# A graph layer on one core: edge groups on TensorE in pairs, with one code and one branch per pair

## The chip, the core and the metric

The kernel runs on one core of a Trainium2 chip. The metric is the device time of one execution in microseconds. Times inside the profile are counted from the start of the span. TensorE's granted clock is given as a share of full speed.

## What is computed

One layer of a graph network on x (625 nodes, 256 channels) with 20000 edges sorted by their target node dst. Cut to what matters:

```python
xn = _layernorm(x)
sums   = segment_sum(xn[src], dst, 625)
counts = segment_sum(ones, dst, 625)
aggr   = sums / maximum(counts, 1)
x = x + (aggr @ W_l.T + xn @ W_r.T + b_r) + linear_attention(xn)
x = x + mixture_of_experts(_layernorm(x))
```

The attention has 8 heads of 32 channels (norms of q and k, second-order terms, projection). The last part is a hidden layer of 1024 with gelu, a softmax over 8 experts and the best expert's matrix for each node, times its probability. Everything is computed in one launch.

## The kernel before

All work is written by hand in five programs, one per engine, that meet in semaphores. The nodes stand in T = 5 tiles of 125. The part of interest is the edge stage. It builds a 625 x 625 matrix of edge counts in PSUM, which is later multiplied with xn @ W_l.T. The 20000 edges are 160 chunks of 125 edges, in NG = 32 groups of GC = 5 chunks. For each chunk, two tiles with one row per edge are made: one marks the edge's target node (VectorE, L644, 628 columns), one is a step at its source node (ScalarE for three chunks of five, L480; VectorE for the other two, L647). TensorE multiplies them: for one tile of target nodes, five chunks, each as a product of 501 columns (L928) and one of 126 columns (L930), adding up in PSUM banks 0 to 6. Since the edges are sorted, most groups have targets in one tile of 125 nodes only. Four of the 32 have a second tile (L938, L940).

**The code.** Which tile a group has is known only at run time. GpSimd makes a code for each group (L432 to L449): first tile + 8 x last tile if that is another + 128 if there are more than two. `group(g)` (L919) loads the code of its group into a register with `value_load` (L921), waits until the fills are there (`oh_ready` from VectorE, `steps_ready` from ScalarE), issues the ten products at addresses taken from the register, and then branches: `If(code > 7)` around the second tile, inside it `If(code > 127)` around a loop over the tiles between. A closing product of two columns (L952) adds 1 to `oh_free`.

**The buffers.** `oh` holds OHB = 7 groups. `fill(g)` on ScalarE (L484) and on VectorE (L639) writes buffer g % 7 and first waits for `oh_free` of at least g - 6:

```python
            def fill(g):
                if g >= OHB:
                    act.wait_ge(oh_free, g - OHB + 1)
                step_rows(g, 0, act_steps(g)).then_inc(steps_ready, 1)
```

**The jobs.** Between the groups TensorE does 14 small jobs for the attention in PSUM bank 7. In this order: the sums M over k (L962, 20 products of 129 columns), five times four transposes of q and k (T, L969), four products U (L986), four products N for the norms (L991). Before job n (from the first T on) it waits for `b7_free`, the reading of the job before. M and U are read by VectorE (L704, L714), T and N by ScalarE (L524 and L532). The order on TensorE is: groups 0 to 2, M, groups 3 and 4, T, groups 5 and 6, T, and so on, two groups behind each job (`groups_to`, L955), then group 31. On ScalarE and VectorE the order of fills is set by `groups_past(job)`: behind the reading of job n come the fills of groups 7 + 2n and 8 + 2n. The engine that does not read a job fills without waiting for it. Behind the last group seven products (L996) end the sums in each bank and release everything that follows (`A_done`): the copies out of PSUM (L539, L723), the attention scores (L1017) and the rest.

## Time and profile before

| | |
|---|---|
| median of 3 runs | 276.13 us (275.94 to 276.99) |
| the profiled execution | 274.62 us |
| its span | 272.9 us |
| TensorE products busy | 238.6 us, 87% of the span |
| VectorE busy | 146.2 us, 54% |
| ScalarE busy | 144.0 us, 53% |
| TensorE's granted clock over the span | 0.998 |
| group 0's first product | 31.94 us |
| closing products of the edge stage (L996) | 106.50 us |

The profiled execution is a single one with the profiler on; its time is its own and lies 1.5 us under the median. PE is TensorE's products, PEld its weight loads, DVE VectorE, ACT ScalarE, POOL GpSimd. A busy time of products contains their pipelined ends, so consecutive rows overlap; the distance between two starts is what one product costs. Register operations, branches, waits and the loading of registers have no rows of their own: they show only as the time in which the array has nothing.

### The profile page before, as it was taken

The numbers are of one execution on the slowest core, as the hardware profiler recorded it, in microseconds if no ns is written. First come the engines' busy times: TensorE is split into PE (matmuls) and PEld (weight loads), VectorE is DVE, ScalarE is ACT, GpSimd is POOL, SyncE is SP. The second block draws the span as 40 slices with busy tenths as digits, with TensorE's granted clock in tenths as the row PEclk, the third lists the DMA queues.
The fourth block names the chain that finished last, engine by engine and source line by source line (L and its number), as shares of the span: only waits on it lengthen the run. The fifth ranks groups of instructions, "written<-read, shape, count | busy, mean of one in ns | idle before, by whom it ended". The sixth has DMA issues, their size and how long they took to land.

```text
span 272.9 us, 4760 instructions
## 1 busy us (share of the span) xinstructions
PE 238.6 (87%) x1447; PEld 146.5 (54%) x1448; DVE 146.2 (54%) x418; ACT 144.0 (53%) x213; POOL 29.1 (11%) x57
## 2 busy tenths in 40 slices
PE   7599799879898998788889997699789999999990
PEld 3248465545454544322227885354445558888880
DVE  2897989996999922973014446900460123322221
ACT  2699656899998952788884011432304332333100
POOL 7018000000000003300000000000053000000331
PEclk9999999999999999999999999999999999999999
DMA  4750000000000000059940000020012300000011
GB/s 127 262 199 2 0 4 2 2 6 2 2 2 2 2 2 2 2 213 424 420 179 2 1 0 0 0 113 40 0 38 65 95 0 4 0 1 2 21 37 40
DMA packets 6032, 15.83 MB, mean 58 GB/s; under 512 B 2725, under 2 KB 3784, under 8 KB 4724
## 3 DMA queue, kind: packets, MB, share of 16 engines
q1 hardware_dynamic: 4576, 13.43, 13.2%
q0 software_dynamic: 1280, 1.31, 1.8%
q10 hardware_dynamic: 144, 0.66, 0.6%
q8 instruction: 22, 0.36, 0.6%
q14 instruction: 10, 0.07, 0.1%
HBM read 14.08 MB, written 1.30 MB: 56 GB/s over the span
## 4 chain that ended last, share of the span: by engine, by line
PE 65%; DVE 17%; ACT 11%; issue 3%; DMA 2%; POOL 0%; DVEq 0%; ACTq 0%
PE ps L1193 15%; PE ps L1128 10%; DVE mem L644 9%; PE ps L887 6%; PE ps L1017 6%; ACT qk_sb L548 6%; PE ps L928 5%; PE ps L1089 4%; DVE mem L647 4%; ACT mem L480 3%; PE ps L1176 3%; DMA edges_sb<-in_edges 2%; PE ps L1080 2%; PE ps L1082 2%; PE ps L1099 2%
## 5 line engine op out<-in xcount | busy, mean ns | idle before, releaser
L480 ACT ACTIVATE mem<-ids_m,half_src 125x628 bf16<-125x628 f16 x96 | 69.9, 808 | 4.4 <-DVE half_src L618 3.6
L928 PE MATMUL ps<-mem 125*128 125x501 bf16 x160 | 47.3, 375 | 11.1 <-issue 6.1
L644 DVE TENSOR_SCALAR mem<-node_ids,dst_f 125x628 bf16<-125x628 f16 x160 | 52.5, 382 | 0.0
L1193 PE MATMUL ps<-mem 128*125 x192 | 41.6, 379 | 0.0
L1193 PEld LDWEIGHTS ps<-mem 128*125 128x125 f32 x192 | 35.9, 188 | 5.4
L930 PE MATMUL ps<-mem 125*128 125x126 bf16 x160 | 35.0, 219 | 0.0
L548 ACT ACTIVATE qk_sb<-ps,sc_col 125x626 f32<-125x626 f32 (+1 forms) x40 | 29.1, 778 | 6.3 <-PE ps L1017 6.3
L928 PEld LDWEIGHTS ps<-mem 125*128 x160 | 15.6, 98 | 29.9 <-issue 17.6
L1128 PE MATMUL ps<-xnT,w_sb 128*128 128x512 f32 (+1 forms) x104 | 28.8, 435 | 1.9 <-ACT mem L579 1.9
L647 DVE TENSOR_SCALAR mem<-ids_m,src_f 125x628 bf16<-125x628 f16 x64 | 24.5, 383 | 0.0
L1128 PEld LDWEIGHTS ps<-xnT,w_sb 128*128 128x128 f32 x104 | 15.9, 191 | 14.7 <-issue 12.6
L582 ACT ACTIVATE mem<-ps,b_sb 128x625 f32<-128x625 f32 x14 | 11.0, 783 | 19.9 <-PE ps L1128 19.6
L1017 PE MATMUL ps<-mem 32*125 32x313 f32 (+1 forms) x160 | 16.1, 472 | 5.1 <-ACT qk_sb L548 5.1
L599 ACT COPY mem<-mem 128x1000 f32 x8 | 8.2, 1031 | 19.8 <-PE ps L1193 19.8
L930 PEld LDWEIGHTS ps<-mem 125*128 x160 | 15.5, 97 | 2.7 <-issue 0.6
L858 DVE SCALAR_TENSOR_TENSOR row<-vz,row x12 | 5.8, 485 | 20.0 <-issue 20.0
L463 POOL DMA_INDIRECT rows_sorted<-row,pos x5 | 6.2, 1235 | 89.9 <-issue 89.9
L1037 PE MATMUL ps<-qk_sb,vz 125*32 125x313 f32 (+1 forms) x160 | 14.7, 439 | 0.9 <-ACT qk_sb L548 0.9
L843 DVE COPY mem<-mem 128x500 f32 (+2 forms) x12 | 4.1, 393 | 20.3 <-ACT mem L582 20.0
L1017 PEld LDWEIGHTS ps<-mem 32*125 32x125 f32 x160 | 6.2, 180 | 16.3 <-ACT qk_sb L548 14.4
L887 PE MATMUL ps<-wqkv_sb,xnT 128*125 128x512 f32 (+1 forms) x40 | 14.1, 490 | 0.0
L744 DVE SCALAR_TENSOR_TENSOR yT_sb<-ps,vs,mem 128x313 f32<-128x313 f32 (+1 forms) x4 | 2.2, 544 | 20.1 <-PE ps L1037 20.1
(200 smaller groups left out, 283.6 us busy)
## 6 DMA issues: line engine op xcount, KB each, us to landing
mem<-in_wd SPq DMA_DIRECT2D x8, 1024.0 KB, 13.1
w_sb<-in_w SPq DMA_DIRECT2D x1, 1024.0 KB, 8.6
vz<-in_bd SPq DMA_DIRECT2D x1, 1000.0 KB
wqkv_sb<-in_w_qkv SPq DMA_DIRECT2D x1, 768.0 KB, 4.2
x_all<-in_x ACTq DMA_DIRECT2D x1, 640.0 KB, 4.8
row<-rows_sorted SPq DMA_DIRECT2D x1, 579.7 KB
wlr_sb<-in_w_lr SPq DMA_DIRECT2D x1, 512.0 KB, 6.0
bqk_all<-in_b_qk SPq DMA_DIRECT2D x1, 256.0 KB, 5.2
```

What stands on the lines that cost most here:

```text
L480: ins = nc.scalar.activation(oh[:, g % OHB, 0, j, :], ids_m1[:, :], ACT.Sign, bias=half_src[:, g * GC + j:g * GC + j + 1])
L548: nc.scalar.activation(gsq[:, u % NGB, :, 0:w], ps[0:TP, b:b + 2, 0:w], ACT.Square, bias=sc2_col[0:TP, :]).then_inc(g_ready, 1)
L582: ins = nc.scalar.activation(hT[:, k, :], psf[:, at:at + N], ACT.Gelu, bias=b1_sb[:, k:k + 1])
L644: ins = nc.vector.tensor_scalar(oh[:, g % OHB, 1, j, :], node_ids[:, :], dst_f[:, col:col + 1], None, ALU.is_equal)
L647: ins = nc.vector.tensor_scalar(oh[:, g % OHB, 0, j, :], ids_m1[:, :], src_f[:, col:col + 1], 2.0, ALU.is_ge, ALU.mult)
L887: ins = mm(ps[0:TP, QKV_BANKS[n % 4], lo:hi], xnT[:, c, TP * t:TP * (t + 1)], w[:, c, :], start=(c == 0), stop=(c == KC - 1))
L928: mm(psf[:, bass.ds(first * BANK, TW + 1)], node_of, oh[:, buf, 0, j, 0:TW + 1], start=False, stop=False, skip_group_check=True)
L930: mm(psf[:, bass.ds(first * P + 5 * BANK, AW)], node_of, oh[:, buf, 0, j, TW:N + 1], start=False, stop=False, skip_group_check=True)
L1017: ins = mm(ps[0:TP, 2 * ((2 * u2 + h // 2) % SLOTS) + h % 2, 0:hi - lo], kT[rows, hg, TP * m:TP * (m + 1)], qT[rows, hg, lo:hi], start=Tru ...
L1037: ins = mm(ps[D * h:D * (h + 1), 6 + k % 2, 0:hi - lo], v[:, m, P * hg + D * h:P * hg + D * (h + 1)], gsq[:, (2 * u2 + pr) % NGB, i, 0:hi ...
L1128: ins = mm(psf[:, at + lo:at + hi], w1_sb[:, c, P * k:P * (k + 1)], x2nT[:, c, lo:hi], start=(c == 0), stop=(c == KC - 1))
L1193: ins = mm(ps[0:TP, 4 + n % EB, 0:C], hT_step[:, n % EB, k, :], wd_sb[:, bass.ds(e, 1), k, :], start=(k == 0), stop=(k == KH - 1))
```

## The change

Groups are taken two at a time. GpSimd packs two codes into one number (code of the even group + 256 x code of the odd one), 16 numbers instead of 32, with two more operations. On TensorE `pair(p)` takes the place of `group(g)`: one `value_load`, the ten products of each of the two groups, then one branch that is taken around the extra tiles of both groups unless a bit of 0xF8F8 is set. Inside, `other_tiles` looks at each half by itself. One closing product per pair adds 2 to `oh_free`. FIRST goes from 3 to 4, so two pairs stand ahead of M, one pair behind M and one behind each other job, and no single group is left at the end. The fills' order moves by one group: 8 + 2n and 9 + 2n behind job n (AHEAD = OHB + 1). The waits for `oh_free` keep their values.

The diff:

```diff
--- before.py
+++ after.py
@@ -26,6 +26,7 @@
     NCH = edges.shape[2]
     GC = 5
     NG = NCH // GC
+    NP = NG // 2
     OHB = 7
     OHW = TP * (T - 1) + P
     H = temp.shape[1]
@@ -106,7 +107,8 @@
         two_code = sb("two_code", [1, NG])
         more_code = sb("more_code", [1, NG])
         ones_col = sb("ones_col", [TP, 1], BF16)
-        flags = sb("flags", [1, NG], I32)
+        pair_hi = sb("pair_hi", [1, NP])
+        flags = sb("flags", [1, NP], I32)
         more = sb("more", [1, T, NG], I32)
         at_sb = sb("at_sb", [P, T * N])
         QB = P + 1
@@ -320,17 +322,20 @@
 
 
         QKV_BANKS = (7, 4, 5, 6)
+        PAIR = 256
         JOB_M = 0
         JOB_QKT = JOB_M + 1
         JOB_U = JOB_QKT + T
         JOB_N = JOB_U + 4
         JOBS = JOB_N + 4
-        FIRST = 3
+        FIRST = 4
+        assert NG == 2 * NP and NG == FIRST + 2 * JOBS
+        AHEAD = OHB + 1
         halves = [(hg, hf) for hg in range(2) for hf in range(2)]
 
 
         def groups_past(job):
-            return [g for g in (OHB + 2 * job, OHB + 2 * job + 1) if g < NG]
+            return [g for g in (AHEAD + 2 * job, AHEAD + 2 * job + 1) if g < NG]
 
         def x_bank(j):
             return ps[:, 4 + j, :]
@@ -445,7 +450,10 @@
             step(nc.gpsimd.tensor_scalar(between[:, :, :], between[:, :, :], 0.0, None, ALU.is_gt))
             step(nc.gpsimd.tensor_scalar(tile_of[:, :, :], tile_of[:, :, :], 0.0, None, ALU.is_gt))
             step(nc.gpsimd.tensor_tensor(tile_of[:, :, :], tile_of[:, :, :], between[:, :, :], ALU.mult))
-            nc.gpsimd.tensor_copy(flags[:, :], two_code[:, :])
+            by_pair = two_code[:, :].rearrange("o (p w) -> o p w", w=2)
+            step(nc.gpsimd.tensor_scalar(pair_hi[:, :], by_pair[:, :, 1], float(PAIR), None, ALU.mult))
+            step(nc.gpsimd.tensor_tensor(pair_hi[:, :], pair_hi[:, :], by_pair[:, :, 0], ALU.add))
+            nc.gpsimd.tensor_copy(flags[:, :], pair_hi[:, :])
             nc.gpsimd.tensor_copy(more[:, :, :], tile_of[:, :, :]).then_inc(flags_ready, 1)
 
             pool.wait_ge(A_done, 1)
@@ -516,7 +524,8 @@
                     act.wait_ge(sums_ready, 1)
                     nc.scalar.activation(nrm[:, :, 0, :], nrm[:, :, 0, :], ACT.Sqrt, scale=SC2)
                     nc.scalar.activation(nrm[:, :, 1, :], nrm[:, :, 1, :], ACT.Sqrt).then_inc(std_ready, 1)
-            fill(T + 1)
+            for g in range(T + 1, AHEAD):
+                fill(g)
 
             fill_past(JOB_M)
             for j in range(T):
@@ -695,7 +704,7 @@
                 scale = nrm[:, t].rearrange("p w (b h) -> p (w b) h", h=HG)[:, :, :, None]
                 nc.vector.tensor_tensor(q4, q4, scale.broadcast_to([TP, 4, HG, D]), ALU.mult
                                         ).then_inc(qk_scaled, 1)
-            for g in range(3, OHB):
+            for g in range(3, AHEAD):
                 fill(g)
 
             dve.wait_ge(b7_full, JOB_M + 1)
@@ -916,45 +925,40 @@
                 zeroed(b)
             pe.wait_ge(flags_ready, 1)
 
-            def group(g):
+            def products(g, tile):
                 buf = g % OHB
-                code = pe.value_load(flags[0:1, g:g + 1], min_val=0, max_val=2048)
-                first = nc.s_assert_within(code & 7, min_val=0, max_val=T - 1,
-                                           skip_runtime_bounds_check_because="each group has edges, each of a tile")
-                pe.wait_ge(oh_ready, g + 1)
-                pe.wait_ge(steps_ready, g + 1)
                 for j in range(GC):
-                    node_of = oh[:, buf, 1, j, bass.ds(first * TP, P)]
-                    mm(psf[:, bass.ds(first * BANK, TW + 1)], node_of, oh[:, buf, 0, j, 0:TW + 1],
+                    node_of = oh[:, buf, 1, j, bass.ds(tile * TP, P)]
+                    mm(psf[:, bass.ds(tile * BANK, TW + 1)], node_of, oh[:, buf, 0, j, 0:TW + 1],
                        start=False, stop=False, skip_group_check=True)
-                    mm(psf[:, bass.ds(first * P + 5 * BANK, AW)], node_of, oh[:, buf, 0, j, TW:N + 1],
+                    mm(psf[:, bass.ds(tile * P + 5 * BANK, AW)], node_of, oh[:, buf, 0, j, TW:N + 1],
                        start=False, stop=False, skip_group_check=True)
 
-                with pe.If(code > 7):
-                    second = nc.s_assert_within((code >> 3) & 15, min_val=0, max_val=T - 1,
-                                                skip_runtime_bounds_check_because="a second tile is there")
-                    for j in range(GC):
-                        node_of = oh[:, buf, 1, j, bass.ds(second * TP, P)]
-                        mm(psf[:, bass.ds(second * BANK, TW + 1)], node_of, oh[:, buf, 0, j, 0:TW + 1],
-                           start=False, stop=False, skip_group_check=True)
-                        mm(psf[:, bass.ds(second * P + 5 * BANK, AW)], node_of, oh[:, buf, 0, j, TW:N + 1],
-                           start=False, stop=False, skip_group_check=True)
-                    with pe.If(code > 127):
+
+            def other_tiles(g, own):
+                with pe.If(own > 7):
+                    products(g, nc.s_assert_within((own >> 3) & 15, min_val=0, max_val=T - 1,
+                                                   skip_runtime_bounds_check_because="a second tile is there"))
+                    with pe.If(own > 127):
                         with pe.Fori(1, T) as t:
                             there = pe.value_load(more[0:1, bass.ds(t, 1), g], min_val=0, max_val=E)
                             with pe.If(there > 0):
-                                for j in range(GC):
-                                    node_of = oh[:, buf, 1, j, bass.ds(t * TP, P)]
-                                    mm(psf[:, bass.ds(t * BANK, TW + 1)], node_of, oh[:, buf, 0, j, 0:TW + 1],
-                                       start=False, stop=False, skip_group_check=True)
-                                    mm(psf[:, bass.ds(t * P + 5 * BANK, AW)], node_of, oh[:, buf, 0, j, TW:N + 1],
-                                       start=False, stop=False, skip_group_check=True)
+                                products(g, t)
+
+
+            def pair(p):
+                code = pe.value_load(flags[0:1, p:p + 1], min_val=0, max_val=PAIR * PAIR - 1)
+                for g, own in ((2 * p, code), (2 * p + 1, code >> 8)):
+                    first = nc.s_assert_within(own & 7, min_val=0, max_val=T - 1,
+                                               skip_runtime_bounds_check_because="each group has edges, each of a tile")
+                    pe.wait_ge(oh_ready, g + 1)
+                    pe.wait_ge(steps_ready, g + 1)
+                    products(g, first)
+                with pe.If((code & 0xF8F8) > 0):
+                    other_tiles(2 * p, code & (PAIR - 1))
+                    other_tiles(2 * p + 1, code >> 8)
                 mm(ps[:, 6, 256:258], zeros[:, 0:P], zeros[:, 0:2], start=False, stop=False,
-                   skip_group_check=True).then_inc(oh_free, 1)
-
-            def groups_to(job):
-                for g in range(FIRST + 2 * job, min(FIRST + 2 * job + 2, NG)):
-                    group(g)
+                   skip_group_check=True).then_inc(oh_free, 2)
 
             def sums():
                 for hg in range(2):
@@ -970,28 +974,26 @@
                                               qk[:, t, part, 0:P], ident[0:TP, 0:TP])
                 ins.then_inc(b7_full, 1)
 
-            for g in range(FIRST):
-                group(g)
+            for n in range(FIRST // 2):
+                pair(n)
             pe.wait_ge(qk_scaled, T)
             pe.wait_ge(consts_ready, 1)
             sums()
-            groups_to(JOB_M)
+            pair(FIRST // 2 + JOB_M)
             for j in range(T):
                 pe.wait_ge(b7_free, JOB_QKT + j)
                 transposed_qk(j)
-                groups_to(JOB_QKT + j)
+                pair(FIRST // 2 + JOB_QKT + j)
             for j, (hg, hf) in enumerate(halves):
                 lo, hi = HALF[hf]
                 pe.wait_ge(b7_free, JOB_U + j)
                 mm(ps[:, 7, 0:hi - lo], MA[:, hg, :], qT[:, hg, lo:hi], start=True, stop=True).then_inc(b7_full, 1)
-                groups_to(JOB_U + j)
+                pair(FIRST // 2 + JOB_U + j)
             for j, (hg, hf) in enumerate(halves):
                 lo, hi = HALF[hf]
                 pe.wait_ge(b7_free, JOB_N + j)
                 mm(ps[:, 7, 0:hi - lo], blk[:, :], uq[:, hg, lo:hi], start=True, stop=True).then_inc(b7_full, 1)
-                groups_to(JOB_N + j)
-            for g in range(FIRST + 2 * JOBS, NG):
-                group(g)
+                pair(FIRST // 2 + JOB_N + j)
             for b in range(7):
                 ins = mm(ps[:, b, 0:2], zeros[:, 0:P], zeros[:, 0:2], start=False, stop=True, skip_group_check=True)
             ins.then_inc(A_done, 1)
```

On TensorE, at the boundary between group 0 and group 1 (`ps` is PSUM, `mem` holds the fills' buffers, `flags` the codes). Before, the program has at that place, behind the skipped extra tiles:

```order
L950 MATMUL ps<-mem 128x126
L945 UNCONDITIONAL_BRANCH
L943 REGISTER_ALU
L943 COMPARE_AND_BRANCH
L942 UNCONDITIONAL_BRANCH
L952 MATMUL ps<-zeros 128x2
L921 TENSOR_LOAD flags
L921 ISA x2
L928 REGISTER_ALU [waits steps_ready,oh_ready]
L928 ISA
L928 REGISTER_ALU
L928 MATMUL ps<-mem 128x501
```

After the change, between the same two groups:

```order
L932 MATMUL ps<-mem 128x501
L934 MATMUL ps<-mem 128x126
L932 REGISTER_ALU [waits steps_ready,oh_ready]
L932 REGISTER_ALU
L932 ISA
L932 REGISTER_ALU
L932 MATMUL ps<-mem 128x501
L934 ISA
L934 MATMUL ps<-mem 128x126
```

The load of the code, the branch and the closing product have gone from this place; they now stand behind the second group of the pair. The branch itself skipped 45 printed rows before and skips 93 now.

On ScalarE, between the last fill before the first job and the first T copy (`mem<-ps` is the copy; three L480 rows, the first with its wait, are one group). Before:

```order
L480 ACTIVATE mem<-ids_m,half_src 125x628 x3
L480 ACTIVATE mem<-ids_m,half_src 125x628 [waits oh_free]
L480 ACTIVATE mem<-ids_m,half_src 125x628 x2
L480 ACTIVATE mem<-ids_m,half_src 125x628 [waits oh_free]
L480 ACTIVATE mem<-ids_m,half_src 125x628 x2
L524 COPY mem<-ps 128x500 [waits b7_full]
```

After:

```order
L488 ACTIVATE mem<-ids_m,half_src 125x628 x3
L488 ACTIVATE mem<-ids_m,half_src 125x628 [waits oh_free]
L488 ACTIVATE mem<-ids_m,half_src 125x628 x2
L488 ACTIVATE mem<-ids_m,half_src 125x628 [waits oh_free]
L488 ACTIVATE mem<-ids_m,half_src 125x628 x2
L488 ACTIVATE mem<-ids_m,half_src 125x628 [waits oh_free]
L488 ACTIVATE mem<-ids_m,half_src 125x628 x2
L533 COPY mem<-ps 128x500 [waits b7_full]
```

Four groups (6 to 9) stand ahead of the first copy in place of three (6 to 8). On VectorE, in the same way, group 7 goes ahead of the reading of M.

## Rows read from the trace of the kernel before

**Rows 1.** The page: the span, and the chain that ended last by line.

```profile
span 272.9 us, 4760 instructions
...
PE ps L1193 15%; PE ps L1128 10%; DVE mem L644 9%; PE ps L887 6%; PE ps L1017 6%; ACT qk_sb L548 6%; PE ps L928 5%; PE ps L1089 4%; DVE mem L647 4%; ACT mem L480 3%; PE ps L1176 3%; DMA edges_sb<-in_edges 2%; PE ps L1080 2%; PE ps L1082 2%; PE ps L1099 2%
```

**Rows 2.** The page, costliest groups: busy us, mean ns | idle before, releasers.

```profile
L480 ACT ACTIVATE mem<-ids_m,half_src 125x628 bf16<-125x628 f16 x96 | 69.9, 808 | 4.4 <-DVE half_src L618 3.6
L928 PE MATMUL ps<-mem 125*128 125x501 bf16 x160 | 47.3, 375 | 11.1 <-issue 6.1
```

**Rows 3.** Windows: each engine busy (instructions), PE clock, DMA share, GB/s.

```profile
60.00:80.00 20.00, 17.47 (x119) 9.79 (x119) 17.61 (x60) 19.86 (x29) 0.00 (x0) 1.00 0.01 2
```

**Rows 4.** Timeline of PE, groups 7 to 9: start, us, instruction, [idle before].

```profile
49.04 0.37 PE L928 MATMUL ps<-mem 125*128 125x501 bf16 x1
...
50.40 0.16 PE L952 MATMUL ps<-zeros 125*128 125x2 bf16 x1
51.24 0.37 PE L928 MATMUL ps<-mem 125*128 125x501 bf16 x1 [0.68 <-DVE mem L647]
...
52.63 0.62 PE L969 MATMUL ps<-ident,qk_sb 125*128 125x125 f32 x4
53.35 0.37 PE L928 MATMUL ps<-mem 125*128 125x501 bf16 x1
```

**Rows 5.** Timeline of PE, group 6 from its second tile on.

```profile
46.95 0.37 PE L938 MATMUL ps<-mem 125*128 125x501 bf16 x1
...
48.30 0.16 PE L952 MATMUL ps<-zeros 125*128 125x2 bf16 x1
```

**Rows 6.** Timeline of PE, sums to group 4.

```profile
37.66 2.48 PE L962 MATMUL ps<-qk_sb 125*128 125x129 f32 x20
39.98 0.38 PE L928 MATMUL ps<-mem 125*128 125x501 bf16 x1
...
41.36 0.37 PE L928 MATMUL ps<-mem 125*128 125x501 bf16 x1
```

**Rows 7.** Timeline of PE weight loads, last zeroing to group 0.

```profile
30.62 0.33 PEld L868 LDWEIGHTS ps<-zeros 125*128 125x128 bf16 x3 [0.95 <-ACT vz L514]
31.91 0.10 PEld L928 LDWEIGHTS ps<-mem 125*128 x1 [0.96 <-issue]
```

**Rows 8.** Timeline of ACT: fills (L480, three per group) and bank copies.

```profile
33.51 4.41 ACT L480 ACTIVATE mem<-ids_m,half_src 125x628 bf16<-125x628 f16 x6 [0.80 <-PE ps L952]
43.39 0.58 ACT L524 COPY mem<-ps 128x500 f32<-128x500 f32 x1 [5.47 <-PE ps L969]
43.87 4.36 ACT L480 ACTIVATE mem<-ids_m,half_src 125x628 bf16<-125x628 f16 x6
...
63.88 21.39 ACT L480 ACTIVATE mem<-ids_m,half_src 125x628 bf16<-125x628 f16 x30
...
91.28 0.51 ACT L532 ACTIVATE mem<-ps,base_col 128x312 f32<-128x312 f32 x1
91.69 4.36 ACT L480 ACTIVATE mem<-ids_m,half_src 125x628 bf16<-125x628 f16 x6
```

**Rows 9.** Timeline of DVE: two fills begin, and the first U.

```profile
40.72 1.25 DVE L644 TENSOR_SCALAR mem<-node_ids,dst_f 125x628 bf16<-125x628 f16 x4
...
42.76 1.26 DVE L644 TENSOR_SCALAR mem<-node_ids,dst_f 125x628 bf16<-125x628 f16 x4
...
67.77 0.55 DVE L714 SCALAR_TENSOR_TENSOR yT_sb<-ps,ks,mem 128x313 f32<-128x313 f32 x1 [2.38 <-PE ps L986]
```

**Rows 10.** Timeline of PE: the last group and the closing products.

```profile
105.11 0.37 PE L928 MATMUL ps<-mem 125*128 125x501 bf16 x1 [0.57 <-issue]
...
106.50 0.31 PE L996 MATMUL ps<-zeros 125*128 125x2 bf16 x7
```

**Rows 11.** Timeline of POOL: the cast that ends the flag work.

```profile
27.23 0.31 POOL L449 CAST more<-tile_of 1x160 int32<-1x160 f32 x1
```

**Rows 12.** The page, DMA queues: packets, MB, share of 16 engines.

```profile
q8 instruction: 22, 0.36, 0.6%
```

## The prediction, made before the changed kernel ran

> **What bounds the kernel now.** The page comes first: the span, and the chain that ended last by line [rows 1]. The chain names VectorE's fills (L644, L647) and ScalarE's (L480) for some 16% of the span, so it is tempting to call the edge stage bound by the fills. The costliest groups say otherwise: the wide edge product L928 stood idle for 11.1 us in all before its 160 starts, and ScalarE's fills waited 0.8 us for a buffer in the whole run [rows 2, 8]. The stretch of 60 to 80 us shows ScalarE at 19.86 of 20 us, VectorE at 17.61, TensorE at 17.47, clock 1.00 [rows 3]: three engines nearly full, so the order of time must tell who is late.
>
> The timeline of TensorE tells it. Groups 7 and 8 are one pair between two jobs. Group 7 starts at 49.04, its closing product (L952) at 50.40, group 8 at 51.24: 1.36 us of products, then some 0.8 us in which the array has nothing. The release is put down to VectorE's L647, but group 8's fill on VectorE began at 42.76 and takes 2.04 us [rows 4, 9]: it had been done for over 6 us. After group 8 stands a job, four transposes, and group 9 follows 0.72 us after they begin, with nothing lost [rows 4]. Such a pair takes 4.31 us (49.04 to 53.35); there are 14 of them, plus groups 0 to 2 and group 31. The gap inside a pair is what TensorE's sequencer needs to get to the next group: load the code from SBUF, branch, make addresses. The job after the second group hides it. The first group after the 20 products of the sums shows the same: group 4 starts 1.38 us after group 3, no gap, since the sequencer had run ahead during 2.3 us of sums [rows 6].
>
> So TensorE is late from 32 to 106.50 us, where the closing products that release everything behind them run [rows 10]. What comes after does not touch the change and should move as a block.
>
> **What the gap is made of.** The ten products of a second tile add 1.36 us (46.95 to 48.30) with no gap before them [rows 5]; they need registers and addresses, but no load of a code. The job's transposes also wait on a semaphore and start at once behind the closing product [rows 4]. What is left is the load of the code and the branch. Before group 0 there is a load with no branch: the last zeroing was released at 30.62 and the first weights came at 31.91, 1.29 us [rows 7]. So the load with the register work behind it is worth between 0.8 us (the gap alone) and 1.3 us. Inside a new pair there is neither load nor branch, only a shift, a mask and waits: I cost it at nothing, as in rows 5, with 0.1 us as the upper end.
>
> **TensorE after the change.** A pair is 2 x 1.35 + 0.03 = 2.73 us, a pair with a job 2.73 + 0.72 = 3.45 us instead of 4.31. Four groups have a second tile, 1.36 us each as before. At one of the 15 boundaries the sums (2.32 us) stand in the job's place, 1.6 longer. TensorE alone would then reach the end of the stage at 31.94 + 15 x 3.45 + 1.6 + 2.73 + 4 x 1.36 = 93.5 us. That is 13 us earlier, and it will not be had, because of what is late next.
>
> **What is late next: ScalarE.** A fill costs it 21.39 / 10 = 2.14 us per group; a copy of transposed q and k costs 0.48 us, of a norm 0.41 us [rows 8]. Per pair that is 4.28 us, with a copy 4.7: more than TensorE's 3.45. It starts with this load when the first job is there. In TensorE's new order: group 0 at 31.94, pair 0 closed at 34.7, one exposed load 0.8, pair 1 closed at 38.2, sums 2.3 [rows 6], groups 4 and 5 at 40.5 to 43.2, first job done at 43.9 (43.39 before). From there ScalarE has 5 copies x 0.48, 22 fills (groups 10 to 31) x 2.14 and 3 norm copies x 0.41: 2.4 + 47.1 + 1.2 = 50.7, up to 94.6 us. Then TensorE needs the third norm copy for its last job. From that release to the last pair's first product I take 1.2 us (job 0.6 to 0.7, and a load only half covered by it; 1.29 in [rows 7] is the upper end), so 95.8; two groups 2.73: the closing products at 98.5 instead of 106.5. **Gain 8.0 us.**
>
> VectorE stays ahead: at worst its group 8 starts at 40.72 + 2.04 (one more fill goes before the sums' readers); 24 fills x 2.04 and four U products x 0.5 end at 93.8 [rows 9]. Its wait of 2.38 us for the first U goes, since two more fills now stand ahead of it.
>
> **Buffers given back in pairs.** Group 7 waits for pair 0, closed at 34.7, where it waited for group 0 alone: ScalarE's fill moves from 33.51 to 34.9. Group 9 moves ahead of the first copy and needs pair 1 (38.2); ScalarE comes to it at 39.2. Three fills end at 41.3, and the copy is at 43.9: the 5.47 us of idle time there [rows 8] covers both. Later a filler is never more than six groups ahead of what has been closed: group 13 on ScalarE would start at about 51 and needs pair 3, closed at about 48. I cost it at nothing; without that cover it would be 1.4 us once per pair.
>
> GpSimd's two added steps on 16 numbers come before the codes are cast; each is less than the 0.31 us of the cast of 160 numbers, so the codes are there by 28.2, and TensorE is busy zeroing till after 30.62 [rows 11, 7]: nothing.
>
> The profiled run took 274.62 us, the median of the runs is 276.13, 1.5 above it; I take the difference of 8.0 from the median: **268.1 us**.
>
> **The rivals.**
> (A) Fills bound the stage, as above: 266.8 to 269.5, the spread being the size of the load (0.8 or 1.3, twice exposed) and ScalarE's rate (1% of 50 us).
> (B) A boundary between pairs costs more than one between groups: two masked halves, nested branches in the four pairs with a second tile, and no lead left on the sequencer. With x us more at each boundary but the one with the sums, which hide it, TensorE ends at 93.5 + 14x; it passes ScalarE's 98.5 from x = 0.36 and the old 106.5 from x = 0.93. At the middle, x = 0.65, it is 102.6, or 272.2 us. For it: the sequencer has no lead after a single job. Against it: the second tile's branch cost nothing visible [rows 5].
> (C) Slower: the branch of a pair without a second tile now skips the extra tiles of both groups, 93 printed rows of code instead of 45, and could end outside the code already fetched. The profile prices a fetch: 22 instruction packets took 0.6% of 16 x 272.9 us, 1.19 us each [rows 12]. If every boundary but the sums' paid that, the stage would end at 93.5 + 14 x 1.19 = 110.2 us, 3.7 later: 279.8 us. It decides from x = 0.93, as in (B). Against it: 0.36 MB in 22 packets is 16 KB a packet for the whole program [rows 12], so new code comes in once in several groups, while today's gap stands behind every group that has no job behind it and is alike each time. The Trainium skill (Runtime: NRT & Kernel Launch, section on instruction fetch mechanics) says that a taken branch whose target lies outside the current window of two 16 KB pages must wait for a fetch of the target page, and counts 256 instructions to a page. By that rule a skip of 93 rows mostly stays inside, but where it does not, the price of (C) is paid; no row here shows such a wait.
> (D) No change: the gap belongs to each group's waits for its two fill semaphores, not to the load. Then it stays inside the pair, TensorE keeps 4.3 us per pair, and the time is 276 us. Releases put down to L647 [rows 4] speak for it; the job's own wait, which costs nothing there, against.
>
> **Chances.** A 0.76, B 0.13, C 0.05, D 0.06. No change means within 0.5% (1.4 us), about what a measurement of this kernel can tell. Faster takes A and nearly all of B, 0.89; same D, 0.06; slower C, 0.05. The range takes A, half a microsecond under it for the spread of a measurement, and the lower half of B: 266.3 to 272.0; the rest of B, C and D is left out, under 0.2.
>
> **What would show it.** Inside a pair the second group's first product follows the first group's last by 0.27 us, no idle time before it. TensorE then waits, before the last groups, for L480's line on ScalarE, which runs without a break from about 44 to 94 us; the idle time before the wide product is no longer "issue". ScalarE's first T copy stands near 43.9, VectorE's last fill ends near 93, the closing products run near 98.5, and from there to the end it is the same 166.4 us. I am wrong if gaps of 0.8 us stay inside pairs (D), if a gap over 0.5 us stands behind a job at a pair's head while its fills are done (B, C), or if a filler stands waiting for buffers after 44 us.

## The result: 268.9 us, and where the stage's gain of 8 us went

The changed kernel takes 268.9 us (267.53 to 270.04, 4 runs) against 276.56 us (275.94 to 277.39, 4 runs) for the kernel before: 0.972 of it, 95% interval 0.967 to 0.977. The forecast was 268.1, in a range of 266.3 to 272.0.

The edge stage, read from group 0's first product to the closing products, took 106.50 - 31.94 = 74.6 us before and 97.73 - 31.34 = 66.4 us now: 8.2 us less. The length repeats from profile to profile: 66.4 us in four profiles of the changed kernel's edge stage and 74.6 in two of the one before, whatever the clock did elsewhere. This is how a pair looks on TensorE now. The timeline of the changed kernel (start, us, instruction, [idle before]; L932 is the wide edge product, L960 the closing product, L973 the four transposes), groups 8 and 9, the job, and the head of group 10:

```profile
48.03 0.37 PE L932 MATMUL ps<-mem 125*128 125x501 bf16 x1 [0.21 <-issue]
...
49.15 0.37 PE L932 MATMUL ps<-mem 125*128 125x501 bf16 x1
...
49.42 0.37 PE L932 MATMUL ps<-mem 125*128 125x501 bf16 x1
...
50.77 0.17 PE L960 MATMUL ps<-zeros 125*128 125x2 bf16 x1
50.80 0.62 PE L973 MATMUL ps<-ident,qk_sb 125*128 125x125 f32 x4
51.73 0.37 PE L932 MATMUL ps<-mem 125*128 125x501 bf16 x1 [0.31 <-issue]
```

Group 9 starts at 49.42, 0.27 us after the last wide product of group 8 (49.15): no gap where [rows 4] show 0.8 us. The pair with its job takes 3.70 us (48.03 to 51.73) instead of 4.31. At the head of most pairs up to 0.4 us of idle time is left, mostly put down to "issue".

The end of the stage on TensorE, and on ScalarE (L488 a fill, L533 a T copy, L541 a norm copy):

```profile
93.10 0.17 PE L960 MATMUL ps<-zeros 125*128 125x2 bf16 x1
93.88 0.79 PE L995 MATMUL ps<-yT_sb,blk 128*128 128x312 f32 x2 [0.61 <-ACT mem L541]
95.00 0.37 PE L932 MATMUL ps<-mem 125*128 125x501 bf16 x1 [0.33 <-issue]
...
97.73 0.31 PE L998 MATMUL ps<-zeros 125*128 125x2 bf16 x7
```

```profile
34.25 6.50 ACT L488 ACTIVATE mem<-ids_m,half_src 125x628 bf16<-125x628 f16 x9 [2.16 <-PE ps L960]
43.32 0.58 ACT L533 COPY mem<-ps 128x500 f32<-128x500 f32 x1 [2.57 <-PE ps L973]
43.79 4.37 ACT L488 ACTIVATE mem<-ids_m,half_src 125x628 bf16<-125x628 f16 x6
48.06 0.56 ACT L533 COPY mem<-ps 128x500 f32<-128x500 f32 x1
...
62.68 21.41 ACT L488 ACTIVATE mem<-ids_m,half_src 125x628 bf16<-125x628 f16 x30
...
93.28 0.54 ACT L541 ACTIVATE mem<-ps,base_col 128x313 f32<-128x313 f32 x1
```

The last job (L995 at 93.88) now waits 0.61 us for ScalarE's copy that begins at 93.28, and ScalarE has had no break since 43.32 [rows 8 show its 5.47 us of waiting ahead of that copy; 2.57 are left]. The page of the changed kernel agrees: the chain that ended last runs over ScalarE's fills instead of VectorE's, and the idle time before the wide product has fallen from 11.1 us [rows 2] to 4.3 (its line now holds the second tiles' products too, so x180).

```profile
span 267.1 us, 4710 instructions
...
ACT mem L488 22%; PE ps L1195 16%; PE ps L1130 12%; PE ps L1019 6%; ACT qk_sb L557 6%; PE ps L1091 4%; PE ps L1178 3%; PE ps L932 3%; PE ps L1082 2%; PE ps L1084 2%; PE ps L1101 2%; DMA edges_sb<-in_edges 2%; DVE qk_sb L705 1%; DVE mem L653 1%; PE ps L1063 1%
...
L932 PE MATMUL ps<-mem 125*128 125x501 bf16 x180 | 50.8, 374 | 4.3 <-issue 2.9
...
L1130 PE MATMUL ps<-xnT,w_sb 128*128 128x512 f32 (+1 forms) x104 | 31.8, 468 | 1.9 <-ACT mem L588 1.9
...
q8 instruction: 21, 0.34, 0.5%
```

**What the stage won and the span did not.** From the closing products to the end it was 272.9 - 106.5 = 166.4 us before and is 267.1 - 97.7 = 169.4 us in this execution. The 3.0 us are in one place, the last group of the page above: the hidden layer's products (L1130) took 31.8 us instead of 28.8. With them the span adds up: 8.2 us won in the stage, 0.6 us because group 0 started earlier, 3.0 lost, 5.8 in all (272.9 to 267.1). The windows of the changed kernel (length, then busy us of TensorE's products, its weight loads, VectorE, ScalarE, GpSimd, then the granted clock):

```profile
160.00:165.00 5.00, 3.81 (x10) 1.72 (x10) 4.58 (x6) 0.81 (x3) 0.00 (x0) 1.00 0.00 0
165.00:170.00 5.00, 3.01 (x10) 1.80 (x11) 3.71 (x4) 3.06 (x6) 0.00 (x0) 0.75 0.04 15
170.00:175.00 5.00, 5.00 (x11) 2.62 (x10) 0.00 (x0) 0.78 (x1) 0.00 (x0) 0.57 0.31 121
175.00:180.00 5.00, 5.00 (x21) 2.82 (x19) 0.00 (x0) 1.57 (x2) 0.00 (x0) 1.00 0.17 72
```

The granted clock went from full speed to half, for 6.8 us in all. It fell between 167 and 168 us, while TensorE stood idle ahead of this block of 32 products, and came back inside it. The block took 11.95 us; the same block took 8.91 us in the kernel before:

```profile
165.07 1.16 PE L1101 MATMUL ps<-xnT,w_sb 128*128 128x125 f32 x8 [0.46 <-ACT xnT L571]
168.15 11.95 PE L1130 MATMUL ps<-xnT,w_sb 128*128 128x512 f32 x32 [1.92 <-ACT mem L588]
```

```profile
173.83 1.16 PE L1099 MATMUL ps<-xnT,w_sb 128*128 128x125 f32 x8 [0.46 <-ACT xnT L562]
176.91 8.91 PE L1128 MATMUL ps<-xnT,w_sb 128*128 128x512 f32 x32 [1.92 <-ACT mem L579]
```

In the two stretches of 5 us that end where the block begins (158.15 to 168.15), TensorE's products were busy for 3.33 and 2.62 us. They were busy for 3.33 and 2.62 us in the same two stretches of the kernel before (166.91 to 176.91). Its windows there show full speed throughout:

```profile
169.00:174.00 5.00, 3.97 (x11) 1.88 (x12) 4.66 (x5) 0.79 (x3) 0.00 (x0) 1.00 0.00 0
174.00:179.00 5.00, 3.08 (x15) 1.94 (x16) 3.47 (x4) 3.04 (x5) 0.00 (x0) 1.00 0.05 16
```

So TensorE's work ahead of the block does not tell the two executions apart. Whether the fall is chance or something that the change shifts had to be tried.

### The profile page after: what moved, and what is told of

Same layout as the page of the kernel before. It is cut to its first block, busy times and chain, and to the rows that moved or that the text cites. A ratio compares the mean times of both kernels' runs of the same rounds, so it can differ in the third digit from the quotient of the medians.

```text
span 267.1 us, 4710 instructions
## 1 busy us (share of the span) xinstructions
PE 240.2 (90%) x1431; PEld 147.0 (55%) x1432; DVE 146.0 (55%) x418; ACT 143.5 (54%) x213; POOL 29.6 (11%) x59
## 4 chain that ended last, share of the span: by engine, by line
PE 56%; ACT 32%; DVE 7%; DMA 2%; issue 1%; POOL 0%; DVEq 0%; ACTq 0%
ACT mem L488 22%; PE ps L1195 16%; PE ps L1130 12%; PE ps L1019 6%; ACT qk_sb L557 6%; PE ps L1091 4%; PE ps L1178 3%; PE ps L932 3%; PE ps L1082 2%; PE ps L1084 2%; PE ps L1101 2%; DMA edges_sb<-in_edges 2%; DVE qk_sb L705 1%; DVE mem L653 1%; PE ps L1063 1%
## 5 line engine op out<-in xcount | busy, mean ns | idle before, releaser
L488 ACT ACTIVATE mem<-ids_m,half_src 125x628 bf16<-125x628 f16 x96 | 69.8, 820 | 5.1 <-DVE half_src L627 2.9
L932 PE MATMUL ps<-mem 125*128 125x501 bf16 x180 | 50.8, 374 | 4.3 <-issue 2.9
L934 PE MATMUL ps<-mem 125*128 125x126 bf16 x180 | 39.3, 218 | 0.0
L1130 PE MATMUL ps<-xnT,w_sb 128*128 128x512 f32 (+1 forms) x104 | 31.8, 468 | 1.9 <-ACT mem L588 1.9
L932 PEld LDWEIGHTS ps<-mem 125*128 x180 | 17.6, 98 | 26.8 <-issue 10.3
L1130 PEld LDWEIGHTS ps<-xnT,w_sb 128*128 128x128 f32 x104 | 17.3, 206 | 16.4 <-issue 14.3
L934 PEld LDWEIGHTS ps<-mem 125*128 x180 | 17.4, 97 | 1.5
```

Of the source, the lines that this page charges most:

```text
L488: ins = nc.scalar.activation(oh[:, g % OHB, 0, j, :], ids_m1[:, :], ACT.Sign, bias=half_src[:, g * GC + j:g * GC + j + 1])
L932: mm(psf[:, bass.ds(tile * BANK, TW + 1)], node_of, oh[:, buf, 0, j, 0:TW + 1], start=False, stop=False, skip_group_check=True)
L934: mm(psf[:, bass.ds(tile * P + 5 * BANK, AW)], node_of, oh[:, buf, 0, j, TW:N + 1], start=False, stop=False, skip_group_check=True)
L1130: ins = mm(psf[:, at + lo:at + hi], w1_sb[:, c, P * k:P * (k + 1)], x2nT[:, c, lo:hi], start=(c == 0), stop=(c == KC - 1))
```

## The experiments

**Which part of the change closes the gap: the load or the branch?** Two kernels, each with one of the two. In the first, a pair loads once, and each group branches for itself:

```diff
                     products(g, first)
-                with pe.If((code & 0xF8F8) > 0):
-                    other_tiles(2 * p, code & (PAIR - 1))
-                    other_tiles(2 * p + 1, code >> 8)
+                    other_tiles(g, own & (PAIR - 1))
```

> The changed kernel, but each group of a pair has its own branch again; the load stays one per pair. The stage is read from group 0's first product to the closing products: 74.6 us before, 66.4 us changed. Theory 1, the load of the code is the gap: the branch costs under 0.2 us, which ScalarE's own chain partly hides, so the stage is 66 to 68 us and the second group of a pair follows the first by 1.35 to 1.5 us. Theory 2, the branch is the gap: the second group follows by 2.1 us and the stage is 73 to 75 us.

In the second, each group loads its own code ahead of its products (GpSimd casts 32 codes unpacked, as before), and the pair has one branch:

```diff
-                code = pe.value_load(flags[0:1, p:p + 1], min_val=0, max_val=PAIR * PAIR - 1)
-                for g, own in ((2 * p, code), (2 * p + 1, code >> 8)):
+                codes = []
+                for g in (2 * p, 2 * p + 1):
+                    own = pe.value_load(flags[0:1, g:g + 1], min_val=0, max_val=PAIR - 1)
+                    codes.append(own)
...
-                with pe.If((code & 0xF8F8) > 0):
+                with pe.If((codes[0] & 0xF8) + (codes[1] & 0xF8) > 0):
```

> The changed kernel, but each group loads its own code; one branch per pair, taken from both codes, stays. Theory 1, the load is the gap: the second group follows the first by 2.1 us, the stage is 72 to 75 us. Theory 2, the branch is the gap: 1.35 to 1.5 us, the stage is 66 to 68 us. If both have a part, both kernels lie between 68 and 73.

Measured, from group 0's first product to the closing products, and from the first group of a pair to its second (in pairs behind a job without a second tile):

| | stage, us | second group after, us | time, us |
|---|---|---|---|
| before | 74.6 | 2.1 to 2.3 | 276.6 (median) |
| two loads, one branch | 75.6 | 1.8 to 1.9 | 275.2 |
| one load, two branches | 68.1 | 1.6 to 1.8 | 269.3 |
| changed | 66.4 | 1.36 to 1.40 | 268.9 (median) |

The two in the middle are single runs, and their times hold what the clock did; the stage is the better measure.

The heads of groups 2 and 3 on TensorE, which are one pair, with one load and then with two:

```profile
35.44 0.37 PE L932 MATMUL ps<-mem 125*128 125x501 bf16 x1 [0.69 <-DVE mem L656]
...
37.17 0.37 PE L932 MATMUL ps<-mem 125*128 125x501 bf16 x1 [0.18 <-issue]
```

```profile
35.83 0.37 PE L932 MATMUL ps<-mem 125*128 125x501 bf16 x1 [0.90 <-DVE mem L656]
...
37.65 0.37 PE L932 MATMUL ps<-mem 125*128 125x501 bf16 x1 [0.27 <-issue]
```

The load is the larger part: with it gone, 68.1 us, with the branch gone alone, 75.6. Theory 1 stands, but its price for the branch was too low, and all its bounds were missed by a little: 68.1 us lies just over 68, 75.6 over 75, and the second groups follow after 1.6 to 1.8 and 1.8 to 1.9 us instead of 1.35 to 1.5 and 2.1. Branch and masks of a group show as 0.3 us inside a pair, and taking them away is worth 1.7 us of the stage once the code is packed. Taken away beside two loads they bring nothing; a pair with a job still takes some 4.3 us, since what the second group gains comes back at the head of the next pair (2.4 to 2.6 us behind a job instead of 2.1 to 2.3). I read this as the sequencer's work per pair setting the pace, not the place where it is seen.

The fair comparison for two loads and one branch is the next kernel but one, which has the same order and return of buffers and two branches: 73.9 us. One branch beside two loads is 1.7 us longer than that. The trace puts it at the second tiles: their products come 0.3 to 0.8 us later at each of the four, 2.3 us together, and the rest of the stage is 0.6 us shorter. So one branch for two groups has a price as well, the nested tests inside it.

**The order and the return of buffers, alone.** The kernel before with four groups ahead of the sums and the fills one group earlier:

```diff
-        FIRST = 3
+        FIRST = 4
+        AHEAD = OHB + 1
...
-            return [g for g in (OHB + 2 * job, OHB + 2 * job + 1) if g < NG]
+            return [g for g in (AHEAD + 2 * job, AHEAD + 2 * job + 1) if g < NG]
```

> The kernel before with only the new order: four groups ahead of the sums and group 7 filled ahead of the first job; loads, branches and closing products one per group. My theory: the order brings nothing, 16 gaps of 0.75 us stay, the stage is 74 to 75.5 us. Rival, that the order (no single group left at the end, fills one group earlier) brings a part of the 8.2 us: 70 to 73 us.

And with the buffers given back in pairs besides:

```diff
-                mm(ps[:, 6, 256:258], zeros[:, 0:P], zeros[:, 0:2], start=False, stop=False,
-                   skip_group_check=True).then_inc(oh_free, 1)
+                if g % 2:
+                    mm(ps[:, 6, 256:258], zeros[:, 0:P], zeros[:, 0:2], start=False, stop=False,
+                       skip_group_check=True).then_inc(oh_free, 2)
```

> As order_alone, and buffers are given back in pairs: no closing product after even groups, 2 added after odd ones. My theory: covered by ScalarE's idle time before the first copy, so within 0.5 us of order_alone. Rival, that the late return holds up the fills: 1 us or more longer than order_alone, with waits of L480 for TensorE after 44 us.

Measured: 75.2 us and 73.9 us. The order brings nothing (0.7 us more than before). The return in pairs holds up no fill, as expected, but it is 1.3 us shorter than the order alone, which I had not expected: 16 closing products fewer, 0.08 us each on average, where the array shows 0.03 from the start of one to what follows. My reading is that with a sequencer that is late, a product costs what it takes to issue, but this is not shown: 0.9 of the 1.3 us stand at four places of the stage, 0.15 to 0.3 us each, and not at every pair. So the 8.2 us are made up of -0.7 for the order, 1.3 for the return, 5.8 for one load instead of two (73.9 to 68.1) and 1.7 for one branch. These are prices in this sequence, each from a single profile; the two loads with one branch show that they do not simply add.

**Is ScalarE what bounds the stage now?** One of its functions says how many of a group's five steps it makes:

```diff
         def act_steps(g):
-            return 3
+            return 4 if g >= 10 and g % 2 == 0 else 3
```

> The changed kernel, but in the 11 even groups from 10 on ScalarE makes four of the five steps instead of three (and VectorE one instead of two): 11 x 0.71 = 7.8 us more on ScalarE, 3.2 us less on VectorE. Theory 1, ScalarE's fills bound the changed stage: it grows by 7 to 8 us, to 73.5 to 74.5. Theory 2, TensorE's sequencer still bounds it (3.6 us per pair and more with a second tile) and ScalarE merely keeps up: it grows by what is above ScalarE's slack, and a growth under 4 us would say so.

> The kernel before with the same shift of work. ScalarE had slack there: from its first copy at 43.4, 23 fills, 5 and 3 copies and 7.8 us more end near 104, and TensorE was at its last group at 105.1. The stage stays at 74.6 to 76.5 us. Rival, ScalarE bounded it already: 80 us or more.

Measured: 74.2 us in the changed kernel, 7.8 more for 7.8 us of added work, all of it; 76.8 in the kernel before, 2.2 more, so ScalarE had 5.6 us of slack there. (The second is 0.3 over its bound.) So every microsecond more on ScalarE now lengthens the stage. How far ScalarE is ahead of TensorE as the bound this does not tell; the version with the late fill, below, does. ScalarE's fills in the changed kernel with more on ScalarE, again without a break:

```profile
45.17 0.58 ACT L533 COPY mem<-ps 128x500 f32<-128x500 f32 x1 [2.56 <-PE ps L973]
45.64 5.07 ACT L488 ACTIVATE mem<-ids_m,half_src 125x628 bf16<-125x628 f16 x7
50.62 0.56 ACT L533 COPY mem<-ps 128x500 f32<-128x500 f32 x1
...
67.37 24.94 ACT L488 ACTIVATE mem<-ids_m,half_src 125x628 bf16<-125x628 f16 x35
92.20 0.51 ACT L541 ACTIVATE mem<-ps,base_col 128x313 f32<-128x313 f32 x1
```

**Is the fall of the clock bound to the waits before it?** Products on zeros in the two waits, in both kernels; they go to a bank whose contents nothing reads at that time (the second argument, added to `kept_busy`, is the bank):

```diff
+            pe.wait_ge(x2T_ready, 3)
+            kept_busy(8, 5)
             pe.wait_ge(in_w1, 16)
             pe.wait_ge(in_gate, 48)
             pe.wait_ge(x2T_ready, T - 1)
...
+                    if k == 2 and not again:
+                        kept_busy(8, 7)
                     if k >= 2:
                         pe.wait_ge(h_ready, again * KH + k - 1)
```

> The changed kernel with 16 products on zeros in two places where TensorE waits before the hidden layer (eight before its first product, eight before the third block waits for the first gelu), so that the array is not idle before the stretch in which the clock fell. My theory: of the 8.8 us that the stage gained, 3.0 us were lost because the granted clock fell to half for 6.8 us at about 169 us; with the array kept busy it stays at 1.00 there, and the median is 1 to 3 us under the changed kernel's 268.9, at 266 to 268. Rival, the fall has nothing to do with those waits: it stays in some runs, and the median is 268.5 to 270.

> The kernel before with the same 16 products. Its profile shows no fall of the clock there, so by my theory it gains nothing: 0.995 to 1.003 of before. If it gains over 0.5%, the kernel before lost clock in some runs as well and a part of the change's gain was hidden by that.

Measured: 266.27 us (265.99 to 266.30, 4 runs), 0.962 of before (0.957 to 0.967); and 274.56 us (274.42 to 276.38), 0.994 of before (0.988 to 1.000). Both stages are as they were, 66.4 and 74.6 us. The block of 32 products takes 8.91 us again in the changed kernel:

```profile
166.51 1.89 PE L1108 MATMUL ps<-zeros 125*128 125x512 bf16 x8
168.59 8.91 PE L1132 MATMUL ps<-xnT,w_sb 128*128 128x512 f32 x32 [0.19 <-ACT mem L588]
```

The kernel before gained 0.6%, a little more than I allowed it, with an interval that ends at no gain: its own timed runs on this chip had granted clocks of 0.974 to 0.992, where the profiled run of the first section had 0.998. So both kernels lose to the clock in some runs. With both kept busy the change is worth 274.56 - 266.27 = 8.3 us, which is the stage's 8.2.

The other profiles say more about the fall ahead of this block. From the closing products to the end it is 166.3 to 166.4 us in the kernel before and in all five variants that load a code per group and have no products on zeros. It is 167.8 to 169.4 us in all four profiles of kernels with one load per pair and no products on zeros (the changed kernel twice, one load with two branches, more on ScalarE), and the block takes 10.35 to 11.95 us there instead of 8.91. One of these four reaches the closing products at 107.4 us, later than the kernel before, so it is not simply that the stage ends earlier. With four against six I would not call it chance, but what in the change brings it about stays open.

**A version that goes on from there.** The last pair waits for a copy that stands behind two fills. ScalarE does the last fill behind the copy instead:

```diff
-                fill_past(JOB_N + j)
+                for g in {0: (28, 29), 1: (30,), 2: (31,), 3: ()}[j]:
+                    fill(g)
```

> The changed kernel with the 16 products on zeros and, on ScalarE, the fill of group 31 behind the third norm copy instead of ahead of it. In the changed kernel TensorE waits 0.6 us for that copy before the last job, and the last pair's first product comes 1.9 us after the pair before is closed. With the copy one fill (2.13 us) earlier the last job follows the closing product at once; group 31's fill, then ready near 93.7, is asked for at about 95.4. The stage falls by 0.7 to 1.0 us, from 66.4 to 65.4 to 65.7, and the time from 266.3 (kept busy alone) to 265.2 to 265.7. Rival, TensorE waits for group 31's fill instead: no gain, 266.0 to 266.6.

> The changed kernel with the 16 products on zeros once more, beside the two others on one chip: 266.0 to 266.6, and a granted clock of 0.993 or more in all runs, if the products hold the clock.

> The changed kernel as it is, on the same chip: the runs spread with their clock, 267.3 to 270, each 1.2 to 3.5 us over the one kept busy. Rival, the fall of the clock was a matter of the other chip or of chance: all runs under 267.

Measured, on one chip, six runs of each of the three, in the order of the expectations: 265.38 us (265.25 to 267.03), 0.960 of before (0.955 to 0.966); 267.80 (266.68 to 268.30); 268.80 (266.54 to 269.79); before 276.25 in 11 runs. The stage falls to 65.4 us, 1.0 less: the last job (L996 here) follows the closing product (L961) at once. Without that wait TensorE needs 65.4 us, then (one wait of 0.33 us for VectorE is left in it), and ScalarE held the changed kernel back by 1.0 us.

```profile
94.88 0.17 PE L961 MATMUL ps<-zeros 125*128 125x2 bf16 x1
94.91 0.77 PE L996 MATMUL ps<-yT_sb,blk 128*128 128x312 f32 x2
```

It is the fastest of all kernels run; of its 2.4 us over the kept-busy kernel beside it, the stage explains 1.0. The second is a miss: 267.8 instead of 266.0 to 266.6, with granted clocks of 0.987 to 0.997. In its profile the clock is 1.00 where the products on zeros stand, but it fell at another place, between 10 and 14 us, behind a wait of 2.7 us for VectorE's first rows, where nothing was added, and group 0's first product came at 32.97 us instead of 31.3 to 31.9:

```profile
6.00:8.00 2.00, 0.86 (x5) 0.19 (x2) 1.93 (x12) 1.27 (x3) 0.82 (x5) 1.00 0.55 194
8.00:10.00 2.00, 0.45 (x4) 0.41 (x4) 1.96 (x10) 0.88 (x2) 0.00 (x0) 1.00 0.84 316
10.00:12.00 2.00, 2.00 (x10) 1.22 (x9) 2.00 (x8) 1.78 (x4) 0.00 (x0) 0.78 0.96 347
12.00:14.00 2.00, 2.00 (x3) 0.38 (x2) 0.42 (x2) 1.76 (x3) 0.00 (x0) 0.50 0.36 102
```

The profiles of the version with the late fill and of the changed kernel with more on ScalarE show the same early fall, group 0 at 33.14 and 33.20 us. In these profiles, then, the products held the clock at the place where they stand, and at that place only: the block of the hidden layer keeps full speed in all three profiles that have them. In time the gain is not shown on this chip, since the six runs with them (266.68 to 268.30) and the six without (266.54 to 269.79) overlap. The third expectation came true in part. Of the six runs of the changed kernel two had clocks of 0.996 and 0.998 and took 266.54 and 266.66 us; the others 0.979 to 0.986 and 268.06 to 269.79. Three runs of the kernel before with 0.997 and 0.998 took 274.61, 274.71 and 275.34. Between the means of these, 266.6 and 274.9, lie 8.3 us. So the changed kernel can run without a fall, and neither theory holds alone.

**Rival (C), the length of a skip.** Into the part that each group's branch skips, in the kernel with the new order and return, go 30 products that never run:

```diff
+                    with pe.If(code > 1000):
+                        for again in range(6):
+                            for j in range(GC):
+                                node_of = oh[:, buf, 1, j, bass.ds(second * TP, P)]
+                                mm(psf[:, bass.ds(second * BANK, TW + 1)], node_of, oh[:, buf, 0, j, 0:TW + 1],
+                                   start=False, stop=False, skip_group_check=True)
```

> order_and_return with 30 more products of 501 columns in the part that each group's branch skips (behind a test for a code above 1000, which none has, so they never run; only the four groups with a second tile pass that test). The skip of each of the 32 branches grows by 30 products and their weight loads, from 45 printed rows to some 76, and the program by 960 products. Theory 1, the length of a skip costs nothing: the stage stays at 73.9, up to 74.5 for the four added tests. Theory 2, rival (C) of the prediction, a longer skip leaves the code already fetched: 0.1 us per branch would make 77, a fetch of 1.2 us at every third branch 86 us.

Measured: 82.4 us, 8.5 more than without them (73.9), and 282.0 us in all, slower than the kernel before. Theory 1 falls. The loss is not spread over the branches. Set beside the kernel without the dead code, group by group, most groups follow the one before after 2.1 to 2.3 us as ever, and eight boundaries, two to five groups apart, are 0.5 to 1.3 us longer, 6.9 us together. The wide product is L930 here, L940 and L942 the second tile's products. First the end of group 6 and the head of the next group, then one of the eight, 2.31 us from the last wide product of one group to the first of the next; without the dead code it is 1.0 there:

```profile
48.55 0.22 PE L942 MATMUL ps<-mem 125*128 125x126 bf16 x1
49.59 0.37 PE L930 MATMUL ps<-mem 125*128 125x501 bf16 x1 [0.82 <-DVE mem L649]
```

```profile
57.28 0.37 PE L930 MATMUL ps<-mem 125*128 125x501 bf16 x1
...
59.59 0.37 PE L930 MATMUL ps<-mem 125*128 125x501 bf16 x1 [1.88 <-ACT mem L481]
```

The dead code changes nothing for VectorE and ScalarE, so the releases named there are again only the last semaphores. The instruction queue has 29 packets of 16 KB where the same kernel without the dead code had 21:

```profile
q8 instruction: 29, 0.48, 0.7%
```

```profile
q8 instruction: 21, 0.34, 0.5%
```

Eight packets more, and eight longer boundaries of 0.87 us on average, under the 1.19 us that a packet takes [rows 12]. The four groups with a second tile, which alone pass the added test, are 0.2 to 0.4 us longer behind it, 1.2 us together. The number agrees with the rule of the Trainium skill that the prediction weighed (Runtime: NRT & Kernel Launch, section on instruction fetch mechanics), that a taken branch whose target is not in the window must wait for its page. A wait for a page to land is not what the trace shows, though. At the boundary above, TensorE's products stand still from 57.7 us on, but the only 16 KB packet there starts between 59.0 and 59.1 us and takes longer than the 0.5 us until the product at 59.59. At four of the eight boundaries a packet is on its way in this manner; at the other four none is when the late product starts. So dead code costs time by the page, and how it does stays open.

## Why the prediction was right, step by step

- **TensorE is late before, the fills are not.** Right. ScalarE had 5.6 us of slack, and one load in place of two moved the stage by 5.8 us with the same fills.
- **The gap is the load and the branch, and inside a pair it is nothing.** Right for the pair (1.36 to 1.40 us from group to group). Of the 0.8 us I gave the branch no price of its own; alone it is worth 0.3 us in the gap.
- **A pair with a job, 3.45 us.** Too low: mostly 3.6 to 3.75. I put it to the sequencer, which has only a little lead at the head of a pair. The nested tests did cost, at three of the four second tiles: the first product of the second tile follows by 0.52, 0.74 and 0.83 us instead of 0.27, 1.3 us together. Here it is 0.74, in groups 18 and 19 of the changed kernel:

```profile
70.53 0.37 PE L932 MATMUL ps<-mem 125*128 125x501 bf16 x1
...
71.27 0.37 PE L932 MATMUL ps<-mem 125*128 125x501 bf16 x1 [0.31 <-issue]
```

- **TensorE alone, 93.5 us.** The step that was most mis-sized. From group 0's first product that is a stage of 61.5 us, 13 us won; the version with the late fill shows 65.4, 9.2 won. The 3.9 us between them, waits of TensorE for a VectorE copy included, are rival (B)'s x: 0.28 us at each of 14 boundaries, and from 0.36 on it would have shown in the time. The forecast kept 5.0 us between TensorE and ScalarE, and there was 1.0. That the number stood although TensorE's term was 3.9 us short is in part luck.
- **ScalarE is next.** Right, and the term that made the number: from the first T copy to the third norm copy I counted 50.3 us (its start to its start), measured 93.28 - 43.32 = 49.96. From that release to the last pair's first product I took 1.2 us after the copy; the copy's 0.4 us end at 93.7, the product starts at 95.00: 1.3. Stage forecast 98.5 - 31.9 = 66.6, measured 66.4.
- **VectorE.** Its last fill was to end by 93.8 at worst, its wait for the first U to go. The windows show it at 20.00 of 20 us from 40 to 80, and its copy behind the closing products starts at 98.08 after 5.58 us of waiting, so it was done at 92.5.

```profile
40.00:60.00 20.00, 19.00 (x144) 11.38 (x143) 20.00 (x72) 17.43 (x27) 0.00 (x0) 1.00 0.01 4
60.00:80.00 20.00, 18.91 (x127) 10.39 (x126) 20.00 (x67) 20.00 (x30) 0.00 (x0) 1.00 0.01 3
```

```profile
98.08 1.85 DVE L732 COPY mem<-ps 125x501 f32<-125x501 f32 x3 [5.58 <-PE ps L998]
```

- **Buffers in pairs cost nothing.** Right in sign; that 16 closing products fewer bring 1.3 us to TensorE was not in the sum. It was not missed there because ScalarE bounds the sum.
- **Everything behind moves as a block.** This did not hold: 169.4 us instead of 166.4 in the profiled run, by the clock, and 167.9 in its second profile. It hardly shows in the medians, since the runs of the kernel before lose clock as well (0.984 to 0.998 in the last comparison's eleven).
- **The rivals.** (D) is refuted by the pair without a gap, its waits being still there. (B) was given 0.13 and its mechanism is there, 0.28 us a boundary, too small by 0.08 to decide. (C) was given 0.05 and did not come. It was right that code that is skipped can cost time, but the length of one skip does not set the price: the changed kernel skips 93 printed rows at a branch, the kernel with the dead code some 76, and only the second is slow. The changed kernel's code as a whole is no longer than before (22 instruction packets there, 21 here); that this is what spared it is my inference.

## What to carry to other kernels

When a profile shows the array idle behind a data-dependent step and names a fill that was ready long before, look for what the sequencer does there, and pack it: one load of a register for several pieces of work brought 5.8 us here, one branch for two 1.7 (but beside two loads it cost 1.7), and fewer small products 1.3. Before counting such a gain in full, add up the next engine from its own rows: the forecast for TensorE alone was 13 us, TensorE could have had 9.2, and ScalarE let 8.2 through. When two such sums lie close, look for what each leaves out: the heads of the pairs and the nested tests, at nothing in the forecast, took up 3.9 of the 5.0 us between them. And judge the stage by its own length, since the clock took 1.4 to 3.0 us behind it in four profiles and some 1.4 us ahead of it in three.

## What the runs showed of the hardware that I had not expected

- Code that is never run cost time where TensorE was late: 8 more instruction packets of 16 KB, 8.5 us, of which 6.9 at eight boundaries. The late products did not start when a packet had just landed, so what they waited for is not shown.
- Sixteen closing products of two columns, 0.03 us each on the array, were worth 1.3 us where TensorE was late; the saving stood mostly at four places.
- The granted clock fell to half ahead of the hidden layer in all four profiles with one load per pair and no products on zeros (1.4 to 3.0 us lost), and in none of the six profiles of the other kernels without them, although TensorE's busy time ahead of it was the same to 0.01 us in the two compared. It fell between 10 and 14 us in three profiles, in one of them besides the fall near 175 us. Products on zeros kept it away only where they stood. By the timed runs each kernel runs with a fall or without; what decides it stays open.
